# A fused attention and mixture-of-experts layer: the beginning in four token chunks, the row maxima spread through a DRAM row, and queries split from an SBUF copy

## What is computed

```python
x = L0_attn_x                                    # (1, 2048, 128)
n = _layernorm(x)
qkv = n @ W_qkv + b_qkv                          # 16 heads of 64
k = k + pos_enc
scores = einsum('bqhd,bkhd->bhqk', q, k) / 8
out = einsum('bhqk,bkhd->bqhd', softmax(scores), v)
x = x + out.reshape(b, s, H * D) @ W_out + b_out
```

## Time and profile before

| | us |
|---|---|
| median of 3 runs | 2255.26 |
| lowest, highest | 2247.64, 2261.68 |
| the profiled execution, its own time | 2247.04 |
| its span, first to last instruction | 2245.2 |
| TensorE busy in the span | 2099.1 (93%) |
| VectorE, ScalarE, GpSimd busy | 1741.8, 1757.7, 1226.4 |
| mean granted TensorE clock | 0.974 of full |

### The profile page before, as it was taken

How to read it: one execution, slowest core, us unless ns; L and a number is a source line. 1 busy time by engine, 2 the same in 40 slices (tenths; PEclk the granted TensorE clock), 3 DMA queues, 4 the chain that set the end, 5 groups by cost and what they waited for, 6 DMA issues and landing times.

```text
span 2245.2 us, 35828 instructions
## 1 busy us (share of the span) xinstructions
PE 2099.1 (93%) x12074; PEld 934.2 (42%) x12074; DVE 1741.8 (78%) x2794; ACT 1757.7 (78%) x2387; POOL 1226.4 (55%) x763
## 2 busy tenths in 40 slices
PE   5899999999999999999999999899999999999997
PEld 2444444444444444444444443333333333333334
DVE  5677777787787777777777775789999999999913
ACT  1588888888888888888888888268878888888882
POOL 1477777777777687687687688332113025006003
PEclk8799999999999999999999999679999999999998
DMA  3000000000000000000000000000000000000000
GB/s 119 1 1 1 1 1 1 1 1 1 1 1 1 1 1 1 1 1 1 1 1 1 1 20 1 1 1 1 2 1 1 2 1 6 2 2 6 1 1 10
DMA packets 12270, 11.30 MB, mean 5 GB/s; under 512 B 2112, under 2 KB 10944, under 8 KB 11968
## 3 DMA queue, kind: packets, MB, share of 16 engines
q1 hardware_dynamic: 12096, 9.01, 1.3%
HBM read 7.69 MB, written 1.05 MB: 4 GB/s over the span
## 4 chain that ended last, share of the span: by engine, by line
PE 61%; DVE 16%; ACT 13%; issue 6%; POOL 1%; DVEq 0%; ACTq 0%; POOLq 0%
PE acc_o L523 11%; PE acc_o L644 10%; PE scores L630 9%; PE scores L493 8%; ACT prob L830 6%; DVE mxp L1343 5%; PE ring L468 5%; DVE accp L1377 5%; ACT scores L838 3%; DVE mxp L1449 3%; ACT prob L861 2%; PE ring L689 2%; PE ring L610 2%; PE ring L697 2%; PE ring L542 2%
## 5 line engine op out<-in xcount | busy, mean ns | idle before, releaser
L1008 POOL TENSOR_TENSOR accp<-accp,prob 128x1024 f32<-128x1024 f32 x318 | 809.1, 2544 | 61.7 <-ACT prob L830 22.4
L1343 DVE TENSOR_REDUCE mxp<-ring 128x1 f32<-128x512 f32 x1024 | 648.1, 683 | 176.0 <-PE ring L468 166.3
L861 ACT ACTIVATE prob<-scores 128x512 f32<-128x512 f32 x1024 | 544.1, 599 | 136.0 <-PE scores L630 133.7
L830 ACT ACTIVATE prob<-scores 128x1024 f32<-128x1024 f32 x512 | 520.0, 1016 | 132.0 <-PE scores L493 109.5
L493 PE MATMUL scores<-q_all,k_all 64*128 64x512 f32 x3072 | 556.8, 408 | 6.4 <-ACT scores L838 4.9
L1449 DVE TENSOR_REDUCE mxp<-ring 128x1 f32<-128x512 f32 x789 | 510.1, 683 | 50.2 <-PE ring L610 34.2
L838 ACT ACTIVATE scores<-minus_all 128x1024 f32<-128x1024 f32 x510 | 524.5, 1029 | 26.3
L523 PE MATMUL acc_o<-prob,v 128*64 128x512 f32 x2048 | 497.4, 606 | 0.0
L468 PE MATMUL ring<-k_all,q_all 64*128 64x512 f32 x1024 | 412.3, 438 | 56.2 <-DVE q_all L1329 24.4
L493 PEld LDWEIGHTS scores<-q_all,k_all 64*128 64x128 f32 x3072 | 340.3, 186 | 64.1 <-ACT scores L838 26.1
L630 PE MATMUL scores<-q_all,k_all 32*128 32x512 f32 x1024 | 304.7, 494 | 13.0 <-ACT prob L861 8.8
(11 more groups left out here) (189 smaller groups left out, 1657.4 us busy)
## 6 DMA issues: line engine op xcount, KB each, us to landing
w_all<-w_pairs SPq DMA_DIRECT2D x1, 1344.0 KB, 11.1
pos_sb<-pos SPq DMA_DIRECT2D x1, 1024.0 KB, 5.8
w_sb<-w SPq DMA_DIRECT2D x4, 256.0 KB, 4.6
mrow<-m_rows SPq DMA_DIRECT2D x64, 2.0 KB
w_all<-w SPq DMA_DIRECT2D x1, 1024.0 KB, 5.4
q_all<-m_rows SPq DMA_DIRECT2D x64, 2.0 KB
out<-ff SPq DMA_DIRECT2D x4, 256.0 KB, 2.2
wout_sb<-wout_pairs SPq DMA_DIRECT2D x1, 512.0 KB, 7.6
```

Source lines behind the costliest of these rows:

```text
L830: nc.scalar.activation(prob[:, T % SLOTS1, :, :], sc[T % 2][:, :, :], ACT.Exp, scale=SCALE1).then_inc(exp_done, 1)
L861: nc.scalar.activation(prob2[:, h // 2, T % 2, h % 2, :], sc2[place % 3], ACT.Exp, scale=SCALE2).then_inc(exp2_done, 1)
L1008: nc.gpsimd.tensor_tensor(accp[:, k % 2], accp[:, k % 2], prob[:, T % SLOTS1], ALU.add).then_inc(pool_acc, 1)
L1343: done(nc.vector.reduce_max(mxp1[k % 2][:, h * QT + q, kc:kc + 1], bank[:], AX.X), ("max", k, q, kc, h))
```

## The change

The beginning works chunk by chunk. x is loaded by four DMAs, each with a semaphore. VectorE does variance and normalisation of a quarter of the tokens at a time, TensorE turns a quarter when it is ready, ScalarE instead of VectorE copies the turned tokens, and T, K, V and Q items stand among the couples of chunk 0. V of blocks 2 and 3 and the row bias go to steps 0, 5 and 2 of chunk 0. Ten couples instead of eight run ahead.

The negated maxima reach all partitions by two DMAs, out to a row in DRAM and back as a broadcast into `minus_all`, which has two buffers. The item minus with its two matmuls and two ScalarE copies is gone. `mrow` remains for tiles 0 and 1 alone.

ScalarE copies queries plus bias to `qf` in SBUF, which frees the bank. VectorE makes `qhi` from `qf` by a copy, and `qlo` = `qf` - `qhi`.

In a chunk the items move: Q from step 2 to 1, sums from 1 to 2, fin from 4 to 3, the first K or V from 3 to 4, and the reciprocals of the sums from steps 2, 3, 4, 5 to 3, 4, 5, 5. GpSimd splits the first block of keys after add 10 instead of 8.

```diff
-EARLY1 = 8
+EARLY1 = 10
 def last_item1(k, j):
     c = k % NC
-    if j == 1 and k > 0:
+    if k == 0 and j in (0, 2, 5):
+        return {0: ("V", 0, 2), 2: ("rows",), 5: ("V", 0, 3)}[j]
+    if j == 1 and k + 2 < CHUNKS1:
+        return ("Q", k + 2)
+    if j == (2 if k < LAST1 else 1) and k > 0:
         return ("sums", k - 1)
-    if j == 2 and k + 2 < CHUNKS1:
-        return ("Q", k + 2)
-    if j in (3, 6) and k // NC + 1 < PAIRS:
+    if j in (4, 6) and k // NC + 1 < PAIRS:
...
-    if j == 4 and k + 1 < CHUNKS1:
+    if j == 3 and k + 1 < CHUNKS1:
         return ("fin", k + 1)
-    if j == 5 and k + 1 < CHUNKS1:
-        return ("minus", k + 1)
 def recip_quarters(k, j):
     if k < LAST1:
-        return [j - 2] if 2 <= j < 2 + QT else []
+        return {3: [0], 4: [1], 5: [2, 3]}.get(j, [])
 def start1():
...
-    return ([("T", c) for c in range(NC)] + [("Q", 0), ("K", 0, 0), ("V", 0, 0), ("V", 0, 1), ("K", 0, 1)] + tiles[0]
-            + [("K", 0, 2)] + tiles[1] + [("K", 0, 3), ("V", 0, 2), ("V", 0, 3)] + tiles[2] + [("Q", 1)] + tiles[3]
-            + [("rows",)] + early[:3] + [("fin", 0)] + early[3:] + [("minus", 0)])
+    def between(c, *items):
+        return tiles[c][:2] + list(items[:1]) + tiles[c][2:3] + list(items[1:]) + tiles[c][3:]
+    return ([("T", 0), ("Q", 0), ("K", 0, 0), ("T", 1), ("K", 0, 1)] + between(0, ("T", 2), ("K", 0, 2))
+            + between(1, ("T", 3), ("K", 0, 3)) + between(2, ("V", 0, 0), ("V", 0, 1)) + between(3, ("Q", 1))
+            + [("fin", 0)] + early)
 # ScalarE
-            def rounded_queries(k):
-                p, c = k // NC, k % NC
+            def queries(k):
+                if k > 0:
+                    act.wait_ge(ql_ready, k)
                 wait_full(act, ("Q", k))
-                nc.scalar.activation(qhi[:, c, :], ring[bank_of(("Q", k))][:], ACT.Identity,
-                                     bias=bqk_all[:, p, 0:1]).then_inc(qh_ready, 1)
+                nc.scalar.activation(qf[:], ring[bank_of(("Q", k))][:], ACT.Identity,
+                                     bias=bqk_all[:, k // NC, 0:1]).then_inc(free[bank_of(("Q", k))], 1)
             def seed(T):
                 if T % NT < 4:
-                    for h in range(2):
-                        wait_free(act, ("minus", T // NT, h))
+                    act.wait_ge(m_spread, 16 * (T // NT + 1))
                 act.wait_ge(exp_done, T - 1)
-                nc.scalar.activation(sc[T % 2][:, :, :], minus_all[:], ACT.Copy).then_inc(seeded, 1)
+                nc.scalar.activation(sc[T % 2][:, :, :], minus_all[:, T // NT % 2], ACT.Copy).then_inc(seeded, 1)
 # SyncE
             for k in range(CHUNKS1):
                 wait_free(sp, ("fin", k))
-                for h in range(2):
-                    sp.dma_start(mrow[64 * h:64 * h + 1, k % 2, :].bitcast(F32),
-                                 m_rows[QT * h:QT * (h + 1), :].bitcast(F32)).then_inc(m_dma, 16)
+                if k == 0:
...
+                sp.dma_start(m_dram[k % 2].rearrange("(a n) -> a n", a=2 * QT), m_rows[0:2 * QT, :].bitcast(F32)).then_inc(m_out, 16)
+                sp.wait_ge(m_out, 16 * (k + 1))
+                if k >= 2:
+                    sp.wait_ge(seeded, NT * (k - 1) - 2)
+                sp.dma_start(minus_all[:, k % 2].rearrange("p h n -> p (h n)"),
+                             m_dram[k % 2:k % 2 + 1, :].to_broadcast([128, 2 * CW])).then_inc(m_spread, 16)
 # VectorE
             def q_proj(k):
-                p, c = k // NC, k % NC
-                bank = open_(("Q", k))
+                c = k % NC
+                wait_free(dve, ("Q", k))
+                nc.vector.tensor_copy(qhi[:, c, :], qf[:]).then_inc(qh_ready, 1)
                 dve.wait_ge(qh_ready, k + 1)
-                done(nc.vector.scalar_tensor_tensor(qlo[:, c, :], bank[:], bqk_all[:, p, 0:1], qhi[:, c, :].bitcast(F32),
-                                                    ALU.add, ALU.subtract), ("Q", k))
+                nc.vector.tensor_tensor(qlo[:, c, :], qf[:], qhi[:, c, :].bitcast(F32), ALU.subtract).then_inc(ql_ready, 1)
-                    if j == STEPS1 - 4 and k + 1 < CHUNKS1:
+                    if j == STEPS1 - 5 and k + 1 < CHUNKS1:
                         mred(k + 1)
```

More of the change, by code:

```diff
@@ L147, in use @@
             uses.extend([("max", *it[1:], h) for h in range(2)])
-        elif it[0] == "minus":
-            uses.extend([(*it, h) for h in range(2)])
         else:
@@ L499, in scores @@
                     return
-                if t < 2:
-                    pe.wait_ge(m_dma, 32 * (k + 1))
+                if t == 0:
+                    pe.wait_ge(m_row, 16 * 2)
                 for h in range(2):
-                    nc.tensor.matmul(sc[u][:, h, :], onesw[half(h), :], mrow[half(h), k % 2, :],
+                    nc.tensor.matmul(sc[u][:, h, :], onesw[half(h), :], mrow[half(h), :],
                                      start=False, stop=True).then_inc(sc_ready[u], 1)
-            def minus(k):
-                pe.wait_ge(m_dma, 32 * (k + 1))
-                for h in range(2):
-                    bank = begin(("minus", k, h))
-                    end(nc.tensor.matmul(bank[:], onesw[half(h), :], mrow[half(h), k % 2, :], start=True, stop=True),
-                        ("minus", k, h))
             def values(T):
@@ L556, in item1 @@
                 elif kind == "rows":
+                    pe.wait_ge(pairs_dma, 16 * 4)
                     rows1()
@@ L563, in item1 @@
                     sums(it[1])
-                elif kind == "minus":
-                    minus(it[1])
                 else:
@@ L734, in item2 @@
                     expert_out(*it[1:])
-            pe.wait_ge(ld, 16 * LOADS1)
-            pe.wait_ge(tokens_ready, 1)
+            pe.wait_ge(ident_ld, 16)
             for it in start1():
+                if it[0] in ("Q", "K", "V"):
+                    wait_free(pe, ("T", it[-1]))
                 if it == ("Q", 0):
-                    for c in range(NC):
-                        wait_free(pe, ("T", c))
                     pe.wait_ge(pair0_dma, 16 * 2)
-                elif it == ("rows",):
-                    pe.wait_ge(pairs_dma, 16 * 3)
-                elif it == ("minus", 0):
+                elif it == early_split():
                     pe.wait_ge(blank, 4)
@@ L798, in _, with deviations, tokens1 @@
         def _(act):
-            def deviation(n):
-                act.wait_ge(var_ready, n)
-                nc.scalar.activation(std[:], std[:], ACT.Sqrt).then_inc(std_ready, 1)
+            def deviations(c):
+                act.wait_ge(var_ready, c + 1)
+                cols = slice(c * QT, (c + 1) * QT)
+                nc.scalar.activation(std[:, cols], std[:, cols], ACT.Sqrt).then_inc(std_ready, 1)
+            def tokens1(c):
+                wait_full(act, ("T", c))
+                nc.scalar.activation(xnt[:, c * CW:(c + 1) * CW], ring[bank_of(("T", c))][:],
+                                     ACT.Copy).then_inc(free[bank_of(("T", c))], 1)
             def v_copy(p, b):
@@ L834, in seed @@
                 if T % NT < 4:
-                    for h in range(2):
-                        wait_free(act, ("minus", T // NT, h))
+                    act.wait_ge(m_spread, 16 * (T // NT + 1))
                 act.wait_ge(exp_done, T - 1)
-                nc.scalar.activation(sc[T % 2][:, :, :], minus_all[:], ACT.Copy).then_inc(seeded, 1)
-            def minus_copy(k):
-                for h in range(2):
-                    wait_full(act, ("minus", k, h))
-                    if k > 0:
-                        act.wait_ge(seeded, NT * k - 2)
-                    nc.scalar.activation(minus_all[:, h, :], ring[bank_of(("minus", k, h))][:],
-                                         ACT.Copy).then_inc(free[bank_of(("minus", k, h))], 1)
+                nc.scalar.activation(sc[T % 2][:, :, :], minus_all[:, T // NT % 2], ACT.Copy).then_inc(seeded, 1)
             def copy_o1(k):
@@ L922, in item2 @@
                                          bias=b1_sb[:, e * FT + f:e * FT + f + 1]).then_inc(free[bank_of(it)], 1)
-            deviation(1)
+            for c in range(NC):
+                deviations(c)
             act.wait_ge(pair0_dma, 16 * 2)
@@ L953, in _ @@
                         sums_copy(it[1])
-                    elif it and it[0] == "minus":
-                        minus_copy(it[1])
                     elif it and it[0] == "Q":
-                        rounded_queries(it[1])
+                        queries(it[1])
                     for it in LATE1.get((k, j), []):
@@ L1416, in _ @@
             link(nc.vector.memset(halves[:], -0.5))
-            dve.wait_ge(ld, 16 * LOADS1)
-            norm(1, xn_tok, x1).then_inc(tokens_ready, 1)
-            dve.wait_ge(pair0_dma, 32)
+            token_variances(0)
+            for c in range(1, NC):
+                token_variances(c)
+                normed_tokens(c - 1)
+            normed_tokens(NC - 1)
+            dve.wait_ge(pair0_dma, 16 * 2)
```

(3 more changed lines are left out.)

91 lines of the change are left out of this document (46 added, 45 removed).

## The result

The changed kernel takes 2317.8 us (median of four runs, 2316.7 to 2321.8), against 2258.1 for the one before beside it. The ratio is 1.028, 95% interval 1.024 to 1.031: slower, and outside the range of the prediction (2175 to 2292). The profiled execution has a span of 2315.5 us, 70.3 more than before. The first difference in its profile is the granted clock of TensorE: 0.95 of full over the span, where before it was 0.974.

A forecast was written before the change was run, and what follows sets the result against it. The prediction took TensorE to set the pace. Its terms, -16 (beginning), +8 (chunk 0), +25 (chunks 1 to 29) and -3 (end), gave +14 us on the median 2255.3: 2269 us, 8-in-10 range 2175 to 2292.

The forecast's parts named there:

- The likeliest case: Whole kernel: VectorE's copy and subtraction both wait for GpSimd's adds; +14 us, 2269 us (2252 to 2288), chance 0.52.
- The copy is excluded: VectorE's copy of the queries from SBUF waits for GpSimd's add, showing about 1.2 us, the subtraction 2.8.
- Rival 1: Copy not excluded, or subtraction served before GpSimd's queued add: stall 1.0 us, total -64 us, 2191 us, chance 0.33.
- The stall of 3.6 us: TensorE's fourth maxima matmul of step 2 waits 3.6 us for the first reduction, in every chunk with a Q.
- the minus item: Steps 5 to 6: its removal saves 1.45 us a chunk, matmuls, bank wait and delayed banks together.
- The 1.3 for the waits at the sums and at the bank of Q: TensorE, end of step 1 to K: waits of 0.50 and 0.81 us go, saving 1.3 us a chunk.
- The step that failed: Chunks 1 to 29: a chunk goes from 41.64 to 42.5 us, +0.85 each, +25 us together.
- The beginning: Before the loop: first reductions at 21, negated maxima at 51, loop at 66.5; -16 us, give or take 5.
- Chunk 0: First chunk: takes over two V and the row bias, and its Q stalls 3.6 us; together +8 us.
- The end: Chunk 30, without Q and with four maxima matmuls fewer: -2.9 us, entered as -3 in the sum.
- Rivals 2 and 3: Slower: tile 15's add loses its turn, 2325 us, chance 0.07; DRAM trip not hidden, 2322 us, chance 0.03.
- a reduction not last at that place would break the stall, whatever the lengths: Sign for step 2: if the first reduction isn't behind copy and subtraction, TensorE's stall of 3.6 us breaks.

The follow-up runs named there:

- e3_subtract_later: The changed kernel with VectorE's subtraction moved one couple of reductions after the copy, at step 2; 2189.6 us, 0.974 of the kernel before.

## Why the prediction was wrong

The likeliest case was right about GpSimd and the stall, and left out what follows the stall, the clock. It forecast +14 us between the profiled executions, and +70 were measured.

- **The copy is excluded**: right. 1.10 and 2.72 us against the 1.2 and 2.8 forecast. The row of the normalisation, half the time per column, had been a sound hint. Rival 1 (copy not excluded, -64 us) is refuted by the result; the run without a copy on VectorE, -53 us, shows that its price was about right.
- **The stall of 3.6 us**: 3.33. A chunk of 42.5 at full clock: 42.4, in the two that kept it. That it comes so near is in part luck, as errors cancel: the minus item gave 1.1, not 1.45, the stall is 0.3 shorter, and the usual chunk before was 41.5, not 41.64. The 1.3 for the waits at the sums and at the bank of Q was right: the changed kernel has neither, and 41.5 - 1.1 - 1.3 + 3.33 = 42.4.
- **The step that failed**: "A chunk becomes 41.64 - 1.45 - 1.3 + 3.6 = 42.5, or +0.85. Chunks 1 to 29 have a Q: 29 x 0.85 = +25 us". It is priced at the clock that the earlier trace rows show, 1.00, though a stall far longer than any in those rows was put in. The runs showed that behind it the clock fell in most chunks, for 1.7 to 1.8 us each. Measured +74.9, of which about 26 is the +0.9 of the full-clock chunk, and the rest, 49, the clock. Chunks 1 to 29 before, and changed:

```profile
123.66:1324.93 1201.27, 1136.67 (x6333) 546.17 (x6334) 926.55 (x1302) 1026.46 (x1103) 907.37 (x402) 1.00 0.01 2
119.03:1395.05 1276.02, 1171.08 (x6275) 553.16 (x6274) 1010.68 (x1330) 999.10 (x1045) 913.11 (x402) 0.96 0.04 14
```

The missing 0.04 of 1276 us is some 50 us. The trace of before held two hints. The lower level was there in the beginning, where the granted clock is 0.77 over the first 82 us. And chunk 2, with a wait of 2.5 us at the sums, was 43.8 us long and not 41.5; but it kept the full clock, so it wouldn't have given the price.
- **The beginning**: -15.1 against -16, first reductions at 21.07 against 21, negated maxima at 52.81 against 51, loop at 67.32 against 66.5. **Chunk 0**: +10.5 against +8, as the clock fell there twice. **The end**: 0 against -3. Chunk 30 went from 41.9 to 43.9 us, not down by 2.9, as the clock fell there too, behind waits of 1.66 and 1.04 us for ScalarE's seeds; 2.6 us came back behind the loop, which no run explains.
- **Rivals 2 and 3**: both didn't come. The add of tile 15 takes 1.21 us in all chunks up to 29 but chunk 2, where it had lost its turn before as well, and the DRAM trip is hidden: 3.6 us for the spread, with no wait in step 6.
- The text had said "a reduction not last at that place would break the stall, whatever the lengths". `e3_subtract_later` put two reductions there, and took 5.3% off the time.
- The range took its upper end from the stall 3.6 +- 0.5 alone. A case "the stall also costs clock" was missing among the rivals; it would have been the one on the slower side.

What stays open: why the clock falls behind one stall and not behind an equal one, in the same kernel. The runs give shares of chunks, not the reason. Nor does the length of the idle time decide alone: chunk 2 of the kernel before kept the full clock behind 2.46 us, and with the values moved the clock fell 5 times behind 1.48.

## What to carry to other kernels

A stall of TensorE is not priced by its length alone: where a change puts in a stall longer than those which the profile shows at full clock, carry a case in which the matmuls behind it run at half rate, here 1.7 us on top of 3.3. Before moving a VectorE operation from PSUM operands to SBUF ones, look at what GpSimd runs at that moment, and avoid two such operations back to back where GpSimd has a queue: here the second waited for a whole one of its instructions. If they must stay, put an instruction that gives TensorE its bank between them, or give TensorE its independent matmuls first; here that returned 5.3% and 3.6% of the time before.
